# Attention and experts in one kernel: the keys get a second buffer and are loaded first in a step, the residual's input is loaded behind the stores of weights

## The reference, cut to what matters

```python
x = x + tanh(g_xattn) * xattn(layernorm(x), ctx, ...)
x = x + tanh(g_ffn) * ffn(layernorm(x), ...)

def xattn(x, context, ...):          # 16 heads of 64, 77 context rows and one null key and value
    q = split(x @ Wq) * 64 ** -0.5
    k, v = split(context @ Wkv)      # a null row is put ahead of each
    out = softmax(q @ k.T) @ v
    return layernorm(merge(out) @ Wout) * ln_scale + ln_bias

def ffn(x, ...):                     # 32 experts, each token uses 8, and one shared expert for all
    affinity = sigmoid(x @ Wr + br); top_w, top_i = top_k(affinity, 8)
    return shared(x) + sum(top_w[e] * expert_e(x) for e in top_i)
```

## Time and profile before

| what | value |
|---|---|
| median of 3 runs | 2459.15 us (2449.6 to 2460.57) |
| the profiled execution | 2462.9 us, of which the span of instructions is 2461.2 us |
| PE, DVE, ACT, POOL busy | 89%, 75%, 58%, 50% of the span |
| attention steps, from the first scores of batch 0 to the first scores of batch 31 | 278.39 to 1426.47 us, 31 steps |
| expert pages | from about 1560 us to the end |

### The profile page before, as it was taken

How to read it: one execution, slowest core, us unless ns; L and a number is a source line. 1 busy time by engine, 2 the same in 40 slices (tenths; PEclk the granted TensorE clock), 3 DMA queues, 4 the chain that set the end, 5 groups by cost and what they waited for, 6 DMA issues and landing times. The chain is left out here.

```text
span 2461.2 us, 44099 instructions
## 1 busy us (share of the span) xinstructions
PE 2184.9 (89%) x14386; PEld 2017.7 (82%) x14386; DVE 1839.2 (75%) x4258; ACT 1419.9 (58%) x4098; POOL 1238.5 (50%) x1326
## 2 busy tenths in 40 slices
PE   7999778789889888888888977999999999999995
PEld 7888677779889878888888976888888888888884
DVE  5655347667677667677677777666799999999996
ACT  4433445556556556555555542577777777777771
POOL 1001103466566556556556566000377777777775
PEclk9999878888899889889889888999999999999997
DMA  9998567775675675676566678999999999999997
GB/s 317 318 321 299 157 240 234 243 223 179 206 226 186 200 232 176 201 233 193 200 220 203 203 257 290 346 285 286 316 392 394 391 396 393 393 394 393 396 373 268
DMA packets 393519, 687.31 MB, mean 279 GB/s; under 512 B 136875, under 2 KB 257420, under 8 KB 390828
## 3 DMA queue, kind: packets, MB, share of 16 engines
q1 hardware_dynamic: 344140, 550.21, 65.3%
q0 software_dynamic: 49152, 134.28, 15.4%
HBM read 345.89 MB, written 338.43 MB: 278 GB/s over the span
## 5 line engine op out<-in xcount | busy, mean ns | idle before, releaser
L1704 POOL DMA_INDIRECT parts<-results_dram,kept_index x512 | 527.6, 1031 | 378.2 <-DMA results_dram<-y 219.6
L853 POOL DMA_INDIRECT pages_dram<-rows,kept_index x512 | 517.1, 1010 | 371.0 <-DMA pages_dram<-blank 219.8
L932 ACT ACTIVATE exps<-sim,minus_max 128x78 f32<-128x78 f32 x1024 | 318.5, 342 | 319.5 <-DVE minus_max L1029 319.5
L1029 DVE TENSOR_REDUCE minus_max<-sim 128x8 f32<-128x624 f32 x128 | 103.2, 806 | 306.2 <-PE sim L141 306.2
L139 PE MATMUL sim<-kT_h,qT_h 128*128 128x156 f32 x512 | 176.9, 345 | 168.0 <-issue 163.7
L139 PEld LDWEIGHTS sim<-kT_h,qT_h 128*128 128x128 f32 x512 | 131.7, 257 | 173.9 <-issue 172.1
L1756 ACT ACTIVATE hid_h<-hidden 128x512 fp32r<-128x512 f32 x175 | 110.6, 632 | 240.9 <-DVE hidden L1860 240.9
L1805 DVE SCALAR_TENSOR_TENSOR parts<-parts,kept_weight 128x256 f32<-128x256 f32 x448 | 223.7, 499 | 16.3 <-DMA parts<-dense_dram 2.4
L932 ACT ACTIVATION_READ_ACCUMULATOR exps<-sim,minus_max 128x1 f32 x1024 | 228.0, 223 | 0.0
L1907 PE MATMUL xps<-ident,xin 128*128 128x128 f32 x1272 | 168.8, 276 | 15.5 <-issue 4.5
L141 PE MATMUL yps<-w_l,hid_h 128*128 128x256 f32 x636 | 178.3, 280 | 0.0
(11 more groups left out here) (272 smaller groups left out, 7483.1 us busy)
## 6 DMA issues: line engine op xcount, KB each, us to landing
xin<-pages_dram SPq DMA_DIRECT2D x159, 512.0 KB, 7.6
results_dram<-y SPq DMA_DIRECT2D x159, 512.0 KB, 6.2
w_raw<-in_experts SPq DMA_DIRECT2D x159, 385.0 KB, 6.2
pages_dram<-blank SPq DMA_DIRECT2D x108, 512.0 KB, 7.6
keys_h_dram<-keys_h SPq DMA_DIRECT2D x32, 624.0 KB, 4.9
keys_l_dram<-keys_l SPq DMA_DIRECT2D x32, 624.0 KB, 6.5
kT_h<-keys_h_dram SPq DMA_DIRECT2D x32, 624.0 KB, 5.6
kT_l<-keys_l_dram SPq DMA_DIRECT2D x32, 624.0 KB, 6.8
```

What stands on the lines that cost most here:

```text
L853: pool.indirect_dma_start(dram["pages"], bass.IndirectOffsetOnAxis(ap=kept_index[:, at:at + 1].bitcast(U32), axis=0), buffer(batch)[:, k / ...
L932: last = act.activation(exps[u % 2][:, h, :], scores(u)[:, h // 4, h % 4, :], ACT.Exp, bias=minus_max[u][:, h:h + 1], accum_out=row_sum[u] ...
L1029: dve.tensor_reduce(minus_max[u][:, :].rearrange("p (a h) -> p a h", a=2), scores(u), AX.X, ALU.max, negate=True).then_inc(max_done, 1)
L1704: pool.indirect_dma_start(parts[slot(batch, t)][:, k, :], None, done, bass.IndirectOffsetOnAxis(ap=kept_index[:, at:at + 1].bitcast(U32), ...
```

## The change

The keys get two buffers, `kT[0]` and `kT[1]`, with a semaphore for each (`keys_loaded[b % 2]`), and batch b uses buffer b % 2. SP issues the keys of batch b+1 right behind `x_in`, and the load now waits for the scores of batch b-1 instead of those of batch b. The load of `x_res` moves from that place to behind the store of the routing weights, ahead of fill 2, with its wait on `biased`. The same loads and stores are done, and no engine but SP has its instructions in another order; the matmuls of the scores read the buffer of their batch.

```diff
-    kT = [sb(f"kT_{s}", [P, PAIRS, 2 * J], F32R) for s in "hl"]
+    kT = [[sb(f"kT{i}_{s}", [P, PAIRS, 2 * J], F32R) for s in "hl"] for i in range(2)]
...
-    keys_loaded = sem("keys_loaded")
+    keys_loaded = [sem(f"keys_loaded{i}") for i in range(2)]
...
         def load_keys(batch):
-            for part, name in zip(kT, ("keys_h", "keys_l")):
-                sp.dma_start(part[:, :, :].rearrange("p q j -> p (q j)").bitcast(F32), dram[name][batch]).then_inc(keys_loaded, 16)
+            for part, name in zip(kT[batch % 2], ("keys_h", "keys_l")):
+                sp.dma_start(part[:, :, :].rearrange("p q j -> p (q j)").bitcast(F32), dram[name][batch]).then_inc(keys_loaded[batch % 2], 16)
...
-            if 0 <= b <= B - 1:
-                if b > 0:
-                    sp.wait_ge(biased, b)
-                sp.dma_start(x_res[:, :, :], x_tiles[b]).then_inc(res_loaded, 16)
+            if 0 <= b <= B - 2:
+                if b:
+                    sp.wait_ge(sim_full, UNITS * b)
+                load_keys(b + 1)
             fill_pages(b, 0)
...
             fill_pages(b, 1)
-            if 0 <= b <= B - 2:
-                sp.wait_ge(sim_full, UNITS * (b + 1))
-                load_keys(b + 1)
...
             if 3 <= b <= B + 1:
                 store_weights(b - 3)
+            if 0 <= b <= B - 1:
+                if b > 0:
+                    sp.wait_ge(biased, b)
+                sp.dma_start(x_res[:, :, :], x_tiles[b]).then_inc(res_loaded, 16)
             fill_pages(b, 2)
...
-            pe.wait_ge(keys_loaded, 32 * (b + 1))
+            pe.wait_ge(keys_loaded[b % 2], 32 * (b // 2 + 1))
```

More of the change, by code:

```diff
@@ L1288, in similarity @@
                 last = split_product(pe, sim[u % 2][:, i // 2, (i % 2) * 2 * J:(i % 2 + 1) * 2 * J],
-                                     [t[:, pair, tt * P:(tt + 1) * P] for t in qT], [t[:, pair, :] for t in kT])
+                                     [t[:, pair, tt * P:(tt + 1) * P] for t in qT], [t[:, pair, :] for t in kT[b % 2]])
             last.then_inc(sim_full, 1)
```

## The result

The changed kernel takes 2196.3 us (median of 4 runs, 2194.13 to 2197.97) beside 2459.86 us for the kernel before on the same chip. The ratio is 0.8942, with an interval of 0.892 to 0.8964: it is faster by 263.5 us. The forecast was a gain of 242 us.

The account below looks back on a forecast made before the run. The prediction took PE to be bound by its wait for late keys and the half clock behind it. 2462.9 - 163.7 - 130 + 40 + 12 = 2221, 2217 us on the median's scale; 8-in-10 range 2168 to 2295.

Parts of the forecast that it names:

- Place and cause of the stall: PE's first scores matmul of each step waits for keys, issued late because SP stands at `x_res` until `biased`: 163.7 us.
- Part 1: PE's wait for keys at the first scores of each step goes, as keys are issued a step ahead: gain 163.7 us.
- Part 2: The half clock in the 9.42 us behind each stall goes: 4.2 us a step, gain 130 us.
- Part 3: Attention steps then take 28.8 us, as PE, DVE and POOL hold each other up: 40 us given back.
- The loop of POOL and DVE: POOL's scatters, `weigh`, `biased` and rstd with DVE's `centre` to `statistics(2)`, summed to 27.8 us a step beside PE's 27.5.
- Part 4: Fill 3 lands unwaited for in middle steps; early steps with larger fills are 3 us longer in about four: 12 us back.
- the floor: The time with stall and half clock both gone: 2169 us, with a step of 27.5 us, PE alone.
- Part 5: `x_res` moved in SP's queue to in front of fill 2 waits as long as before or shorter: nothing gained or lost.
- DMA- or POOL-bound steps: Rival: fill 3 lands in 12 us and scatters queue, a step of 30.9 us, 2282 us in all; chance 0.18.
- The clock stayed at 1.00: Against the rival that PE's short waits for DVE keep the clock down, losing the 130 us: 2347 us; chance 0.05.
- The slower case: Rival: keys and values make fill 3 land late, over 18.1 us; at 20 us of landing, 2518 us; chance 0.03.

Follow-up runs that it names:

- e1: Kernel before with only `x_res` moved behind the store of the weights, keys keeping one buffer and their place: 2195.69 us, ratio 0.8933.
- e2: Changed kernel with two key buffers, but the loads of keys and `x_res` put back at their old places: 2456.47 us, ratio 0.9992.
- e4: Kernel before with 36 extra matmuls of 128x256 on PE ahead of its wait for the keys: 2431.07 us, ratio 0.9892.
- e5: Changed kernel without the third product of the scores: 2747.57 us beside a kernel before of 2817.21 on another chip, ratio 0.9777.
- e3: Changed kernel with `x_res` and its wait on `biased` put back ahead of fill 0, behind the keys: 2272.61 us, ratio 0.9248.
- e13: Changed kernel with its fills begun one step earlier: 2758.32 us beside a kernel before of 2758.07 on another chip, ratio 1.0064.

## Why the prediction was right, and where its sizes were off

**Place and cause of the stall: right.** Keys arrive late because SP stands at `biased`. The prediction said "Not because of the one buffer", and e1 and e2 show it: all of the gain without a second buffer, none with the buffer alone.

**Part 1, 163.7 us: right.** The wait at `sim` is gone.

**Part 2, the half clock: right, and a little large.** 3.92 us a step measured against 4.2, so 121 us, not 130. Two slips partly cancel in it. The 44 matmuls at the low clock were priced by the mean of the 183 others, 5.2 us and a factor of 0.56; the same 44 take 4.99 us in the step of the changed kernel that begins at 695.49, a factor of 0.53. And the step that was read had more of the half clock than most: PE was busy for 32.32 us in it, beside 31.58 in the mean of fifteen. Also, parts 1 and 2 are not two gains that could each be had alone: e4 got 28 us from the clock. The sum of both holds for this change because the same move opens the second loop too.

**Part 3, what the step then waits for: over-sized, and the largest error.** I took 28.8 us, "1.3 above PE alone", for engines that hold each other up. The step is 27.76, 0.26 above the 27.5. That is 31 x 1.04 = 32 us too much. The loop of POOL and DVE was summed at 27.8 us, as long as the measured step, so it has to be shown that it is not what bounds it. POOL and then DVE in the middle step of the changed kernel:

```profile
713.62 0.72 POOL L843 TENSOR_TENSOR rstd<-var_eps,minus_half 128x2 f32<-128x2 f32 x1
...
721.56 0.19 POOL L841 TENSOR_TENSOR var_eps<-mean_var,eps_col 128x2 f32<-128x2 f32 x1 [1.92 <-DVE mean_var L1055]
```

```profile
715.02 0.87 DVE L1063 SCALAR_TENSOR_TENSOR z<-ring,mean_var,scale_row 128x256 f32<-128x256 f32 x2
...
721.23 0.25 DVE L1055 BATCH_NORM_AGGREGATE mean_var<-stats 128x2 f32<-128x6 f32 x2
```

POOL's rstd is there at 714.34. `centre` starts at 715.02 without having waited for it, since DVE was busy with other work up to then. So the loop has a slack of 0.7 us and sums to 27.0 in this step, not 27.8. POOL's wait of 1.92 us is inside the loop, while DVE does its part, and is no slack, although the expectation of e5 counted it so. The room under PE is therefore small: by an estimate from these rows, e5 on a chip like that of the change would still have had this loop at about 27.0 us, above the 26.1 to 26.8 that were expected. No run shows it.

**Part 4, the fills: right in the middle, under-sized at the start.** In the middle steps nobody waits for a fill; they land in a median of 3.7 us, not 7.8, though the DMA share rose from 0.64 to 0.83. For the start I gave 12 us for four steps of 3 us. The first six steps take 193.9 us, 27.4 above six of 27.76, which is 15 too little. With part 3 that makes 35.5 us measured above the floor (887.97 less 31 x 27.5) where 52 were foreseen. What failed is the picture that a step with more transfers is longer by itself. It isn't, as long as nobody waits for the fills: step 1 took 26.94 us with a DMA share of 0.91. SP falls behind instead, and the debt is paid in one piece of 25 us in step 3.

**Part 5, `x_res`: right of the new place, silent on the old.** Its wait costs 1.1 us now. What I did not see is that the old place of that wait was itself a loop bound, worth some 73 us in the steps beyond the keys (e3). The prediction needed no such number, since both loads move, but it would have misjudged either half.

The account: 16.5 us less given back than parts 3 and 4 said, 1.9 us more from the floor by rounding, and 4.9 us outside the steps, which the prediction held equal: 23 us between the 2221 of the sum and the 2197.97 of the profiled execution. The 4.9 us (the rest of the span is shorter by 5.9, and the steps begin 1.1 later) are not explained. Part 3 gave back 32 us too much and part 4 some 15 too little; that the forecast of 2217 lies within 21 us of the measured time is in part this cancelling, and luck.

**The rivals.** DMA- or POOL-bound steps needed landings of 12 us. In the middle steps they were at most 5.7; in step 3 the fill that POOL waited for, one of three pages, took 11.8, so something of this rival came true there, once. The clock stayed at 1.00 in the middle steps, with no wait of PE from 500 to 1100 us. The slower case needed a landing of 18.1 us.

## What to carry to other kernels

In a queue that issues in order, look for the longest wait and ask what stands behind it: here one load with a late wait held ten value loads, the keys and the fills, and moving that load alone (e1) gave all that it gave together with a second buffer, a second semaphore and an earlier load of the keys. Before adding a buffer, see whether the wait on the buffer is the one that is met last. When two gains come from one stall, as idle time and a lower clock, follow each loop through all engines and sum it: a second loop of nearly the same length takes up whatever you win on the first.

## What the runs showed of the hardware

The landing of a fill of 512 KB fell from 7.8 to 3.7 us while the share of the DMA engines rose from 0.64 to 0.83. It seems to go with what was issued just ahead, and not with the mean load. In one step of the kernel before, the fill at 861.05, with only `x_res` just ahead of it, took 3.9 us, and the fills at 874.91 and 876.76, behind the keys and the stores, took 7.5 and 8.5. In the middle step of the changed kernel the last fill, at 719.07 behind a store alone, took 3.1.

SP's issues are not of one price. The ten loads of the values took 14.1 us of SP's time in a middle step of the changed kernel, 9.0 us in the same place of e1, and 19.9 us in step 2. The Trainium skill ("DMA: Bandwidth & Descriptors", section "Issuing engines are not separate DMA queues") calls the sequencer's time to start a DMA usually small beside the DMA itself; here the ten take half of a step of 27.7 us, and this time is a term of both loops of the kernel before.

The kernel before took 2456 to 2460 us on the chips of most runs here, and 2758 and 2817 us on two others. In the trace of e13, from one of these, matmuls wait in the midst of the scores, and this kernel, which has the order of the change, was not faster than the kernel before.
